# Query products ahead of the transposes, and one semaphore fewer, in a graph attention kernel

## What is computed

```python
q = (xp @ Wq[l] + bq[l]).reshape(n, H, HD)
k = (xp @ Wk[l] + bk[l]).reshape(n, H, HD)
v = (xp @ Wv[l] + bv[l]).reshape(n, H, HD)
att = jnp.einsum('ehd,ehd->eh', q[dst], k[src]) / scale
att = jnp.clip(att, -50.0, 50.0)
ex = jnp.exp(att - m[dst])                  # m, s: maximum and sum by destination
alpha = ex / (s[dst] + 1e-16)
aggr = segment_sum(v[src] * alpha, dst)
x = x + (aggr @ Wo[l] + bo[l])              # then layer norm and a GELU MLP, also residual
```

## Time and profile before

| what | value |
|---|---|
| median of three runs | 2697.52 us |
| the three runs | 2701.51, 2687.93, 2697.52 us |
| span of the profiled execution | 3472.7 us |
| PE, weight loads, DVE, ACT, POOL busy | 68%, 58%, 57%, 49%, 52% of the span |
| mean granted TensorE clock | 0.807 |

### The profile page before, as it was taken

The page is one execution under the profiler, slowest core; times in us unless marked ns, Lnnn a source line. Parts: engine busy times, 40 slices in busy tenths (PEclk is TensorE's granted clock), DMA queues, the critical chain, the costliest instruction groups (busy, mean ns, idle before and its releaser), DMA issues.

```text
span 3472.7 us, 60241 instructions
## 1 busy us (share of the span) xinstructions
PE 2377.0 (68%) x13853; PEld 2027.0 (58%) x13854; DVE 1981.1 (57%) x7060; ACT 1704.5 (49%) x4472; POOL 1820.8 (52%) x1968
## 2 busy tenths in 40 slices
PE   6998774567667676777667746666666666666667
PEld 6988333556556565656556635556565565565556
DVE  7887782455555555555556625555555455554555
ACT  6765653345445444545445434354444445454444
POOL 5642655655555555555555245556555555555552
PEclk9999885778878878878888867788778778787788
DMA  7865232222322222222223122222222222222221
GB/s 211 242 207 172 88 106 85 85 77 84 89 86 84 84 79 85 79 86 82 82 83 88 45 72 83 82 81 84 81 77 78 81 79 81 77 81 81 78 84 37
DMA packets 180176, 323.48 MB, mean 93 GB/s; under 512 B 38740, under 2 KB 93991, under 8 KB 179892
## 3 DMA queue, kind: packets, MB, share of 16 engines
q0 software_dynamic: 80208, 216.22, 21.7%
q1 hardware_dynamic: 98948, 103.44, 9.7%
q10 hardware_dynamic: 736, 0.93, 0.1%
HBM read 288.09 MB, written 20.71 MB: 89 GB/s over the span
## 4 chain that ended last, share of the span: by engine, by line
another core or an unknown queue 15%; PE 13%; issue 10%; DVE 8%; DVEq 3%; ACT 3%; ACTq 0%; DMA 0%; SPq 0%
PE bank L2080 5%; DVE aggregate L2120 3%; PE bank L2071 2%; PE bank L1729 2%; PE bank L1723 1%; DVE arena L2128 1%; ACT arena L2013 1%; PE bank L2056 1%; PE bank L1720 1%; DVE arena L2148 1%; DVEq L2109 1%; DVE arena L2162 1%; DVEq L2120 1%; PE bank L1718 1%
## 5 line engine op out<-in xcount | busy, mean ns | idle before, releaser
L1992 POOL DMA_INDIRECT arena<-kv_rows,idx_stage x1612 | 1540.8, 956 | 1344.6 <-DVE arena L2128 798.4
L2080 PE MATMUL bank<-arena 128*128 128x136 f32 x3328 | 698.7, 359 | 654.1 <-DVE aggregate L2120 551.8
L2120 DVE TENSOR_TENSOR aggregate<-bank,aggregate 128x136 f32 x1664 | 493.9, 297 | 1017.6 <-remote 851.3
L2080 PEld LDWEIGHTS bank<-arena 128*128 128x128 f32 x3328 | 589.1, 249 | 746.1 <-DVE aggregate L2120 419.9
L2071 PE MATMUL bank<-queries,arena 128*128 x3328 | 547.5, 317 | 82.0 <-DVE arena L2148 53.6
L2071 PEld LDWEIGHTS bank<-queries,arena 128*128 128x128 f32 x3328 | 509.9, 233 | 91.3 <-issue 90.8
L2013 ACT ACTIVATE arena<-iota_n,at_negdst 128x128 f32<-128x128 f32 x1664 | 527.7, 395 | 3.8 <-DMA kv_rows<-arena 2.0
L1777 ACT ACTIVATE arena<-bank 128x256 f32<-128x256 f32 (+1 forms) x225 | 85.0, 379 | 731.8 <-remote 454.8
L2056 PE MATMUL bank<-ident,arena 128*128 128x128 f32 x1664 | 325.7, 329 | 106.1 <-issue 63.0
L2148 DVE TENSOR_TENSOR arena<-bank,arena 128x512 f32<-128x512 f32 x416 | 284.6, 684 | 152.8 <-remote 68.2
L2037 ACT ACTIVATE arena<-arena 128x32 f32<-128x32 f32 x416 | 92.8, 223 | 556.0 <-DVE arena L2177 336.3
(11 more groups left out here) (322 smaller groups left out, 2796.3 us busy)
## 6 DMA issues: line engine op xcount, KB each, us to landing
arena<-in_edge_attr_dram SPq DMA_DIRECT2D x244, 256.0 KB
arena<-kv_rows,idx_stage POOLq DMA_INDIRECT x1612
kv_rows<-arena SPq DMA_DIRECT2D x12, 512.0 KB, 3.8
kv_rows<-arena SPq DMA_DIRECT2D x24, 256.0 KB, 2.2
arena<-in_x_dram SPq DMA_DIRECT2D x12, 256.0 KB, 4.0
x_rows<-arena SPq DMA_DIRECT2D x12, 256.0 KB, 2.9
x_stream<-arena SPq DMA_DIRECT2D x12, 256.0 KB, 2.3
queries<-arena SPq DMA_DIRECT2D x12, 256.0 KB, 2.7
```

Of the source, the lines that this page charges most:

```text
L1992: pool.indirect_dma_start(kv[:, n, :], None, kv_dram[l], bass.IndirectOffsetOnAxis(idx_stage[:, half % 2, n:n + 1], 0)).then_inc(Z.kv_in[s ...
L2080: pe.matmul(sums_of(j), sel[:, r % SEL_SLOTS, j, :], msg[:, r % 2, j, :], start=True, stop=True).then_inc(Z.sum, 1)
L2120: dve.tensor_tensor(a, sums_of(j), a, ALU.add).then_inc(Z.added, 1)
```

## The change

The order of PE's turn becomes: spread of quad k + 2, then transposes of quad k + 4. The spread's last matmul raises no semaphore any more, and `qe` is gone. Whoever waited for it waits for the transposes that are issued right behind it: `selt` now counts the transposes of k + 4 as the sign that both these and the spread of k + 2 have been done. DVE waits before L2148 of quad k for the transposes of k + 2; ACT's `copy_t` has one wait where it had two. At the end of each layer, where there are no quads left to transpose, two single transposes of the identity (`close`) give that sign. The start of a layer issues two quads of transposes, then alternates spread and transposes.

```diff
+        AHEAD = 2
+        def turned(l, k):
+            return l * (AT_QUADS + AHEAD) + k + 1
             def copy_t(k, r):
-                act.wait_ge(Z.selt, k0 + k + 1)
-                if not (isinstance(k, int) and k < SELT_SLOTS):
-                    act.wait_ge(Z.qe, k0 + k - SELT_SLOTS + 1)
+                act.wait_ge(Z.selt, turned(l, k))
...
+            def close(k, r):
+                pe.wait_ge(Z.selt_sb, k0 + k - 1)
+                pe.transpose(bank[:, ATT_BANK[0][r % 2], 0:P], ident[:, :], ident[:, :]).then_inc(Z.selt, 1)
...
                 for j in range(QUAD):
-                    m = pe.matmul(bank[:, ATT_BANK[1][r % 2], j * D:(j + 1) * D], sel_t[:, r % SELT_SLOTS, j, :],
-                                  q_all[:, bass.ds(tiles[j], 1), :].rearrange("p t d -> p (t d)"), start=True, stop=True)
-                m.then_inc(Z.qe, 1)
+                    pe.matmul(bank[:, ATT_BANK[1][r % 2], j * D:(j + 1) * D], sel_t[:, r % SELT_SLOTS, j, :],
+                              q_all[:, bass.ds(tiles[j], 1), :].rearrange("p t d -> p (t d)"), start=True, stop=True)
...
+                    if not (last and r + 2 >= QUADS):
+                        spread(k + 2, r + 2, ahead[r % GROUP * QUAD:])
                     if not (last and r + 4 >= QUADS):
                         transposes(k + 4, r + 4)
-                    if not (last and r + 2 >= QUADS):
-                        spread(k + 2, r + 2, ahead[r % GROUP * QUAD:])
+                    elif r + 2 < QUADS:
+                        close(k + 4, r + 4)
...
-            for n in range(4):
+            for n in range(AHEAD):
                 transposes(n, n)
             begin = load_tiles(0, 2 * QUAD)
             for n in range(2):
                 spread(n, n, begin[n * QUAD:])
+                transposes(n + AHEAD, n + AHEAD)
...
-                    dve.wait_ge(Z.qe, k0 + k + 1)
+                    dve.wait_ge(Z.selt, turned(l, k + AHEAD))
```

More of the change, by code:

```diff
@@ L1943, in __init__ @@
                 self.selt_sb = sem("selt_copied")
-                self.qe = sem("q_spread")
                 self.prod = sem("prod_ready")
```

## The result

The changed kernel takes 2705.53 us, the median of 20 runs (2698.97 to 2711.48), against 2697.82 us for the kernel before in 20 runs (2687.93 to 2705.01). The ratio is 1.0031, with a 95% interval of 1.0022 to 1.0041. Both were measured once more side by side on one chip: 1.0016 (1.0004 to 1.0028). The change costs 4 to 8 us and brings nothing.

The account below looks back on a forecast made before the run. The prediction took POOL's issue of gathers to bound a run. It summed 2697.5 + 0 (semaphore) + 0 (order, covered) + 2 (ends) - about 2 (updates) = 2697 us, range 2640 to 2718.

Parts of the forecast that it names:

- Bound of a run: POOL's issue of 1612 gathers, 1.25 us each without waiting, bounds a run: 2694 to 2704 us in all.
- Why two times stood side by side: Profiled span 3472.7 against 2697.5 us timed: the 775 us were POOL waiting on late PE semaphore updates, nearly absent in runs.
- the prediction's own sign: In the profile after, remote waits before DVE's adds below 200 us and span toward 2702 would show holds gone, runs unchanged.
- Semaphore: nothing: Dropping `qe`, 416 updates fewer on PE and one ACT wait fewer in 412 quads, gains 0 us in a run.
- the rival that the hold only moves: PE's late updates catch the transposes' semaphore instead; profile near 3470 us, run 2697; about half, for the profiled execution.
- Order: covered: Transposes behind the spread on PE delay the sums up to 0.60 us a quad, hidden by POOL's slower pace: 0 us.
- The bound of 250 us without cover: Cost of the new PE order if no slack hid it: 416 x 0.60 = 250 us.
- The 1.11 us of the prediction: Slack a quad by which the unheld PE, DVE and ACT loop (3.73 us) outruns POOL (4.84 us).
- The sum: 2697 us, no change to tell: All terms added give 2697 us; unchanged within about 0.5%, 13.5 us, had chance 0.71.
- the ends: Last 8 quads of each layer, after its last gather, run uncovered: 0 to 10 us, taken as 2 us.
- Faster by holds that vanish: Late PE updates also cost timed runs and the change removes some: 2453 us if half, up to 2684; chance 0.19.
- Slower by the loop as the bound: In 104 quads with PE's heavy dense pieces the loop paces, paying 0.60 us each: 62 us, 2759 us; chance 0.10.

Follow-up runs that it names:

- chip A: Chip of the fast kind used for follow-ups; the unchanged kernel before has a median of 2696 to 2700 us there.
- chip B: Chip of the slow kind on which the unchanged kernel before was profiled and timed once more: 3476.88 us.
- chip E: Chip of the slow kind on which the changed kernel ran beside the kernel before: 3510.43 against 3511.14 us, ratio 0.9995.
- the halved gathers: Kernel before with 48 gathers a body in the place of 62, wrong values: 2996.0 us (0.8506); the same edit on the changed kernel: 2985.32 us (0.8475).
- chip C: Chip of the slow kind, where the kernel before takes 3519.0 us; the weighing product cut in two pieces took 3537.2 us there, in four 3552.22 us.

## Why the prediction was right, and where it was wrong

**Bound of a run.** Right: POOL issues gathers without waiting, 17.7 us in 58 gaps of 0.305 us, and 182 gathers fewer are worth 185 us. The close agreement of its sum was partly luck. The sum had 2015 to 2025 us for the gathers and 79.1 + 60.1 us behind the two layers, all from a chip of the other kind. On chip A the kernel before has 2064.7 us and 57.3 + 35.1 us: 40 to 50 us too little and 47 us too much, which cancel. So "the run has no time left in which a hold could lie" was true there, but the 0.5% agreement was no proof of it.

**Why two times stood side by side.** Wrong. I took the 775 us for something of the profiled execution. On chip B the kernel before took 3476 us in its timed runs as well: it's the chip. The inference on the bound survived because the median gather, 0.946 us, is the same on either kind. "In a run the holds are nearly absent" holds on one of five chips; on four they are there. For the same reason the prediction's own sign would have misled. The profile after has no wait for remote and a span of 2703.3 us, as if the change had removed the holds, and the kernel before has neither holds nor a longer span on chip A.

**Semaphore: nothing.** Not contradicted on either kind. On chip E the rival that the hold only moves is what happened, 0.9995 at 3511 us. I had given it about half, for the profiled execution alone, and on the wrong ground. On chip A its price is not isolated, since the version without it had a matmul more.

**Order: covered.** The bound of 250 us without cover never applied, since POOL was the bound throughout: it has no wait for the loop in the profiles after. The cover that was tested is smaller than the prediction's: in the second layer 4.96 us a quad (1031.4 / 208) is POOL's pace in the kernel before, and 4.39 a pace at which the loop still kept up, so 0.57 us at the least. The 1.11 us of the prediction came from one pair of products at the end of a layer and was not tested.

**The sum: 2697 us, no change to tell.** The measured change is +8 us (+4 in the second pair), within the 0.5% that I had called no change, and inside the range. Yet the interval of 20 runs, 1.0022 to 1.0041, excludes 1, and the sum had the change at 0. The step that failed is the price of the order: "+ 0 (order, covered) + 2 (ends) - about 2 for updates". The order alone, with the semaphore left where it was, measured 1.0039 (1.0025 to 1.0053). The cover kept 250 us away and not the last 4 to 8. Which of the two terms was short is open. One candidate is the gathers: the sum held each at 1.25 us or at a fixed mean, and a gather's length depends on whether DVE's product runs when it starts. The mean is 0.976 to 0.981 us in six profiles of chip A's kind and 0.956 in the profile that I had read. That the shifted loop makes this term larger isn't shown: the order alone had 0.976. The other candidate is the ends, whose bound of 0 to 10 us would hold all of it. The stretch after the last gather was 36.6, 39.7 and 39.9 us with the new order, and 35.1 to 39.9 with the old.

**Rivals.** Faster by holds that vanish: fell, 1.0031 on one kind and 0.9995 on the other. Slower by the loop as the bound: fell as a mechanism, POOL has no waits in the profile after. It had the sign right; its 62 us were some ten times too many.

## What to carry to other kernels

When a profile and the timed runs differ by a quarter, settle first whether both come from the same chip and repeat the unchanged kernel before explaining anything. A sum that meets the measured time may do so because two of its terms are off in opposite directions: compare it stretch by stretch once a profile of the right chip is at hand. A queue that bounds a kernel by issuing back to back isn't immune to the engines beside it. List the duration of its instructions against what ran when they started: here a 0.68 us product delayed one gather in nine, by up to 0.54 us, and cost 48 us of the run. Moving a semaphore from one instruction to its neighbour did nothing where updates were held as a stream.

## What the hardware showed that I had not expected

- On four of five chips PE's semaphore updates reach the other engines late while gathers are issued: the two cases shown are 5 us late, and waits for remote before the adds last up to 9.3 us (the halved gathers on chip C). The kernel before takes 3475 to 3519 us there and 2697 on the fifth. In the profile before, 297 of 300 waits for remote lie between the first and the last gather of a layer. 1336 of the 3171 rises of PE's semaphores that its trace records come more than 1 us after a matmul that could have raised them, against 22 of 3402 on chip A. For DVE it is 37 of 5040 against 32 of 6461, so it is PE's updates that are late. Matmuls at fixed addresses are held as well. With 1248 gathers in the place of 1612 the waits for remote halve. What differs between the chips, and what path is shared, is open.
- A gather issued by POOL takes 0.946 us, and up to 1.5 us if a DVE product with two SBUF operands is running when it starts, by what that product has left less 0.13 us. With one operand in PSUM it is 0.948 us in the mean, and the run takes 48 us less of 2700. A kernel with right values that does this wasn't made.
